# The weighing matmuls of an attention group issued one head earlier in TensorE's order

## What is computed

```python
attn1 = jnp.einsum('bhqd,bhkd->bhqk', q, k)
attn2 = jnp.einsum('bhqd,qkd->bhqk', q, rk2)
attn = jax.nn.softmax((attn1 + attn2) / scale, axis=-1)
w1 = jnp.einsum('bhqk,bhkd->bhqd', attn, v)
w2 = jnp.einsum('bhqk,qkd->bhqd', attn, rv2)
x = (w1 + w2).transpose(0, 2, 1, 3).reshape(B, S, E)
```

## Time and profile before

| | us |
|---|---|
| median of 3 runs | 3290.31 |
| lowest and highest run | 3290.27, 3292.92 |
| the profiled execution's own time | 3288.23 |
| its span | 3286.4 |
| mean granted TensorE clock | 0.934 of full |

### The profile page before, as it was taken

How to read it: one execution, slowest core, us unless ns; L and a number is a source line. 1 busy time by engine, 2 the same in 40 slices (tenths; PEclk the granted TensorE clock), 3 DMA queues, 4 the chain that set the end, 5 groups by cost and what they waited for, 6 DMA issues and landing times.

```text
span 3286.4 us, 50994 instructions
## 1 busy us (share of the span) xinstructions
PE 2703.9 (82%) x15346; PEld 1863.3 (57%) x15346; DVE 1770.5 (54%) x4053; ACT 1241.3 (38%) x2184; POOL 1301.6 (40%) x1038
## 2 busy tenths in 40 slices
PE   0784799878997799868997799977998789977897
PEld 0453556555665556655665556655565556655565
DVE  5523564566456564565545654555545654555635
ACT  0234432373234522363233623354233622354322
POOL 1442244433444254432444245342544334442544
PEclk9997899998999899998998989998999989998999
DMA  7018400671018400671008600482008600294007
GB/s 212 27 51 180 120 1 7 126 200 33 1 52 181 132 1 7 114 200 46 1 30 176 160 1 7 92 187 80 1 8 164 173 21 0 72 185 108 1 7 136
DMA packets 491228, 271.08 MB, mean 82 GB/s; under 512 B 222747, under 2 KB 486772, under 8 KB 487668
## 3 DMA queue, kind: packets, MB, share of 16 engines
q1 hardware_dynamic: 416612, 255.53, 31.2%
q10 hardware_dynamic: 74304, 11.80, 3.7%
HBM read 136.11 MB, written 131.16 MB: 81 GB/s over the span
## 4 chain that ended last, share of the span: by engine, by line
PE 62%; issue 8%; ACT 6%; DVE 5%; DMA 4%; SPq 1%; POOL 1%; ACTq 1%; DVEq 0%; POOLq 0%
PE PS L1501 55%; PE PS L1504 7%; ACT arena L1022 2%; ACT arena L1015 2%; DMA bias_scr<-arena 2%; DMA prob_scr<-arena 1%; DMA q_scr<-arena 1%; DVE PS L1283 1%; SPq L530 1%; POOL rstd L389 1%; DVE arena L1239 0%; DVE nmax L1283 0%; DVE cbn L1206 0%; DVE arena L1228 0%; POOL crs L389 0%
## 5 line engine op out<-in xcount | busy, mean ns | idle before, releaser
L1501 PE MATMUL PS<-arena 128*17 128x128 f32 (+6 forms) x6864 | 816.4, 324 | 81.0 <-ACT arena L1022 61.1
L1504 PE MATMUL PS<-ident,arena 128*128 128x128 f32 (+1 forms) x3406 | 558.2, 294 | 292.2 <-ACT arena L1022 134.2
L1501 PEld LDWEIGHTS PS<-arena 128*17 128x17 f32 (+3 forms) x6864 | 554.6, 129 | 263.3 <-issue 105.2
L1504 PEld LDWEIGHTS PS<-ident,arena 128*128 128x128 f32 (+1 forms) x3406 | 419.0, 150 | 495.5 <-ACT arena L1022 164.7
L1501 PE MATMUL PS<-cwk,arena 128*128 128x512 f32 (+1 forms) x936 | 477.5, 635 | 2.4 <-ACT arena L904 2.4
L389 POOL TENSOR_TENSOR crn<-crn,mhalf 128x8 f32<-128x8 f32 (+1 forms) x234 | 419.1, 1797 | 125.9 <-DVE crn L1220 124.2
L1283 DVE CUSTOM_DVE_ANT_0 PS<-PS,arena 128x512 f32<-128x512 f32 x512 | 344.2, 710 | 175.8 <-PE PS L1501 93.0
L899 ACT ACTIVATE arena<-PS 128x512 f32<-128x512 f32 (+1 forms) x234 | 139.7, 597 | 686.7 <-PE PS L1501 686.7
L1015 ACT ACTIVATE arena<-PS,nmax 128x512 f32<-128x512 f32 x512 | 351.9, 691 | 120.4 <-DVE nmax L1283 94.4
L796 POOL TENSOR_TENSOR arena<-arena,mass_mask 128x512 f32<-128x512 f32 x128 | 163.5, 1277 | 446.7 <-ACT arena L1015 435.6
L1022 ACT ACTIVATE arena<-PS 128x512 f32<-128x512 f32 x384 | 229.5, 598 | 109.2 <-PE PS L1501 103.7
(11 more groups left out here) (158 smaller groups left out, 3733.5 us busy)
## 6 DMA issues: line engine op xcount, KB each, us to landing
arena<-bias_scr SPq DMA_DIRECT2D x130, 336.0 KB, 3.2
prob_scr<-arena SPq DMA_DIRECT2D x128, 336.0 KB, 4.2
bias_scr<-arena SPq DMA_DIRECT2D x132, 256.0 KB, 4.2
q_scr<-arena SPq DMA_DIRECT2D x144, 128.0 KB
arena<-q_scr SPq DMA_DIRECT2D x132, 128.0 KB, 3.4
arena<-k_scr SPq DMA_DIRECT2D x18, 768.0 KB, 11.6
bias_scr<-arena ACTq DMA_DIRECT2D x36, 320.0 KB, 16.1
arena<-prob_scr SPq DMA_DIRECT2D x128, 80.0 KB, 3.7
```

The source lines that it names most:

```text
L1501: return pe.matmul(o, l, r, start=start, stop=stop, **kw)
L1504: return pe.transpose(o, i, ident[0:i.shape[0], 0:i.shape[0]])
```

## The change

In `attn_pe` the call of `weigh` for the group before moves from behind the transposes of head j = 1 to behind those of head j = 0.

```diff
                             transpose_probs(t, h)
-                            if g and j == 1:
+                            if g and j == 0:
                                 weigh(t, g - 1)
                     weigh(t, NG - 1)
```

## The result

| | before | changed |
|---|---|---|
| median of the runs, us | 3290.29 (4 runs) | 3319.57 (4 runs) |
| lowest and highest, us | 3282.19, 3292.92 | 3317.85, 3319.91 |
| span of the profiled execution, us | 3286.4 | 3318.1 |
| mean granted clock | 0.934 | 0.934 |

The changed kernel is slower: 1.0085 of the kernel before, with a 95% interval of 1.0052 to 1.0118. That is 29.3 us between the medians and 31.7 between the profiled spans. Of the runs further down, one of the four of e4_reorder is a slow one, 4110.87 us at a granted clock of 0.647, and its figures leave it out.

What follows compares the result with a forecast made beforehand. It took a loop through three engines, with its path through VectorE, as the bound. Terms 33.6 - 2.0 + 3.1 = +34.7 us on 3288.23 gave 3322.9, and 3325.0 for the median; range 3302 to 3356.

Steps and rivals of the forecast that it cites:

- What bounds: Attention stage: no engine is full; a loop through TensorE, VectorE and ScalarE sets the pace, 5.49 us per group.
- What is gained: Moved groups: W starts 0.05 us after E, the end of ScalarE's evac(g-1,3), not 0.64; `pv_done` comes 0.65 us earlier.
- second rival: Moved groups: the earlier `pv_done` is passed on, 0.65 us in each of 80 groups, -52 us, 3238; chance 0.04.
- What is paid: Moved groups: S(g+1,1) and its bias fall behind W, delaying evac(g,1); the next E comes 0.42 us later per group.
- How many: Per batch 10 of 12 moved calls pay, one being last and one hidden in tile 0; 80 in all, +33.6 us.
- The last group: Last group of each batch: W(2) passes T(3,1) alone, gaining 0.25 us, -2.0 us over 8 batches.
- The sum of these: Attention stage: 33.6 us paid in the moved groups less 2.0 gained in the last groups.
- The clock: Tile ends: another TensorE hole of about 0.3 us puts two more tile ends at half clock, +3.1 us.
- first rival: Moved groups fall to half clock too, 1.54 us each: 3356 with 20 of 80, 3448 with all; chance 0.15.
- Nothing absorbs it: Behind the attention stage: the next begins with TensorE and VectorE working on its output, so the +34.7 us arrives.
- The range of its own: Whole time 3312 to 3342: tile ends all at full clock take 20 us off, falls in groups add 15.
- third rival: Moved groups: the delay washes out on VectorE or in waits for DMAs, 3290 to 3297; chance 0.07.

Runs made afterwards that it cites:

- e4_reorder: Against the kernel before: S(g+1,2) and W ahead of T(g,1), three biases before evac(g,1), exp(g+1,1) before evac(g,0); 0.9709 of it, 3213.09 us.
- e1_s_first: Changed kernel with W(g-1) behind S(g+1,1) again, still ahead of T(g,1): 0.9947 of the kernel before, 3288.59 us.
- e2_w_first: Changed kernel with W(g-1) moved ahead of S(g+1,0) too: 1.0336 of the kernel before, 3417.44 us.
- e6_evac_first: Changed kernel with VectorE doing evac(g,1) ahead of bias(g+1,1): 1.0302 of the kernel before.
- e8_no_act_swap: e4_reorder with ScalarE's old order, so only TensorE's and VectorE's lists differ from the kernel before: 0.9733 of that kernel.
- e10_before_fill: Kernel before plus eight matmuls of zeros ahead of W(3) at each tile end: 0.9900 of the kernel before, 3275.20 us.
- e9_fill_all: Changed kernel plus five matmuls of zeros ahead of each moved W and eight ahead of W(3) at tile ends: 1.0003 of the kernel before, 3304.18 us.
- e11_fill_again: e9_fill_all repeated unaltered beside e10_before_fill: 0.9982 of the kernel before, 3301.47 us.
- filled pair: e10_before_fill and e11_fill_again, both with zeros filling TensorE's holes, differing by the order alone: 3275.20 and 3301.47 us.
- e3_fill: Changed kernel plus five matmuls of zeros ahead of each moved W, none at tile ends: 1.0061 of the kernel before, 3323.46 us.

## Why the prediction was right

It forecast 3325.0 us with a range of 3302 to 3356, slower by 34.7; measured were 3319.57 and 29.3. Its steps, one by one:

- **What bounds.** Right. It took the loop through VectorE as the bound and not an engine's busy time. The busy times didn't change, and the groups took what the list behind W said in e1_s_first, e2_w_first, e6_evac_first and e8_no_act_swap (5.37, 6.53, 6.27 and 4.57 us). The whole times did so less well, as the clock came on top.
- **What is gained.** Right and worthless, as forecast. W starts at E+0.05; ScalarE is freed at E+1.24 (1.19 forecast) and then waits for `nmax` twice, 0.58 and 0.52 us. The second rival falls with that.
- **What is paid.** 0.42 us per group forecast: evac(g,1) at E+2.27 and the next E at 5.91. Measured are 2.25 and 5.88, that is 0.40 over the 5.48 of before; with the 24 groups of 5.95 the mean over 64, all holes filled, is 0.425 (377.8 - 350.6 = 27.2 us). That the bias put behind W is the cause is shown by e1_s_first, which keeps the early W and loses nothing, and by e2_w_first, where a second bias adds another 0.65.
- **How many.** 80 groups, one per batch hidden behind a landing. With two prices per batch it gave tile 0 a growth of 6.7 us. Against e10_before_fill tile 0 grew by 6.8 us in e9_fill_all and by 8.6 in e11_fill_again, where three full prices would make 10. So something was hidden, by these two traces a third of a group to a whole one.
- **The last group.** -2.0 us forecast. With all holes filled the last distance of a batch is 5.37 us after 5.48 in seven batches and 6.05 in one, so 1.5 us in all. It is a small term, and it was sized from two rows.
- **The sum of these.** 33.6 - 2.0 = 31.6 us for the order alone. The filled pair shows 33.4 inside the attention stages and 26.3 between medians. That the sum fits is more than luck, as its main term fits by itself.
- **The clock.** This is the weak term. +3.1 us was forecast, from two more tile ends at half clock. The count of slow tile ends rose by four, 13 to 17, but each was milder, and their sum didn't grow. What was put aside as the first rival did happen in part: 7 of 64 groups fell to half clock behind a 1.6 us hole. They cost 7.3 us, 1.0 each and not 1.54, and the last groups 2.9. In the stages the two kernels lose 30.3 (755.8 - 725.5) and 18.9 us (711.0 - 692.1) to the clock, in traces of several chips, so the term measures 11.4 there, nearly all of it outside the tile ends; between medians it is 3.0 (29.3 - 26.3), and that this equals the forecast is luck. The Trainium skill, "TensorE: Matmul & The Clock Gate", section "A second HAM failure mode: psum-queue depth-cycling", says that short idles between groups of matmuls make the clock swing between its two levels. The trace agrees for one group in nine behind the 1.6 us holes; behind 1.4 us, in the kernel before and in e1_s_first, none of 64 groups was slow.
- **Nothing absorbs it.** Right, as far as the traces go. In the median 29.3 arrived of the 44.8 us that the profiled attention stages show, and the rest of the span was 13.1 us shorter, in places that the change doesn't touch. But in the filled pair the rest is equal within 0.1 us and all 33.4 us arrive in the span. That points to scatter between executions: the rest lies anywhere from 2562 to 2585 us in the thirteen traces, and the runs of one kernel on one chip differ by up to 31 us. It isn't proved for the first pair.
- **The range of its own.** The forecast's 3312 to 3342 does not follow from its terms: all tile ends at full clock take 20 us off 3325.0, which is 3305. The measured 3319.57 lies inside either way.

The third rival, a wash-out, falls with the group of 5.88 us.

## What to carry to other kernels

When an instruction that waits is moved up in an engine's list, price what it is moved past: work that was done under the old wait goes behind it, and with it everything queued behind its consumers on other engines. The same move is a small gain if the independent work stays ahead of the wait (e1_s_first), and a gain of 2.7 to 2.9%, part of it from the clock, if more of it is put there (e8_no_act_swap, e4_reorder). Read the loop from one handover to the next in the time line before trusting busy shares, and after each gain look for which landing comes last.

## What was not expected of the hardware

Matmuls of zeros kept TensorE's clock up here. Eight of 128x512 in bf16, 1.89 us in the 2.28 us hole at a tile end, left none of 24 tile ends over 6.8 us, where 13 to 17 had been in the unfilled kernels, and gave the kernel before 1.0% (0.9900, 0.9872 to 0.9929) for no useful work.

A deeper hole mostly goes with more falls. Groups longer than usual by over 0.5 us were none of 64 behind 1.4 us (the kernel before, e1_s_first), 7 behind 1.6 (the changed kernel, twice), 9 and 18 behind 2.3 (e6_evac_first, e2_w_first). But the depth alone doesn't decide. Behind the same 2.28 us, tile ends over 6.8 us were 5 of 24 in e2_w_first, 10 in e3_fill, 13 in the kernel before, 16 and 17 in the changed kernel and 19 in e1_s_first. What else decides stays open.
